# Routed experts in a transformer layer: picking by an added mask and a maximum, instead of weighing and summing

## The reference

```python
gates = jax.nn.softmax(xf @ wg, axis=-1)
idx = jnp.argmax(gates, axis=-1)
mask1 = jax.nn.one_hot(idx, E, dtype=x.dtype)
loc = jnp.sum((jnp.cumsum(mask1, 0) - 1.0) * mask1, -1).astype(jnp.int32)
keep = loc < cap
h = jnp.einsum('ecd,edf->ecf', disp, w1) + b1[:, None, :]
y = (jnp.einsum('ecf,efd->ecd', h, w2) + b2[:, None, :]).reshape(E * cap, D)
out = jnp.where(keep[:, None], gate_val[:, None] * y[jnp.minimum(slot, E * cap - 1)], 0.0)
```

## Time and profile before

| what | value |
| --- | --- |
| median of 3 runs | 667.09 us (665.74 to 670.02) |
| the profiled execution's own time | 663.18 us |
| its span, first to last instruction | 661.5 us |
| busy in the span: PE, DVE, ACT, POOL | 525.5, 543.0, 424.8, 229.2 us |
| mean granted TensorE clock | 0.911 |

### The profile page before, as it was taken

One profiled execution on the slowest core, in us unless ns is written; L12 is line 12 of the kernel. 1 busy time (PEld: TensorE's weight loads), 2 busy tenths in 40 slices (PEclk: granted clock), 3 DMA queues, 4 the chain that ended last, 5 costly groups with the idle time before them and its releaser, 6 DMA issues.

```text
span 661.5 us, 9881 instructions
## 1 busy us (share of the span) xinstructions
PE 525.5 (79%) x3439; PEld 208.4 (31%) x3439; DVE 543.0 (82%) x872; ACT 424.8 (64%) x909; POOL 229.2 (35%) x360
## 2 busy tenths in 40 slices
PE   2884799999899999999999986776486675998710
PEld 1570122222222222222222222555466542443300
DVE  4759799999899999999999933798838257899996
ACT  1542489989889888898889873434344403656554
POOL 7000110110133451334513480482344402686761
PEclk9996699999999999999999999887678686999955
DMA  9832011101211112111112001100000000000112
GB/s 247 256 130 113 16 34 26 41 26 46 60 56 39 30 41 63 57 35 34 47 53 60 14 6 27 56 1 1 0 1 1 1 1 0 0 1 0 33 32 63
DMA packets 31285, 28.92 MB, mean 44 GB/s; under 512 B 6132, under 2 KB 23676, under 8 KB 31236
## 3 DMA queue, kind: packets, MB, share of 16 engines
q1 hardware_dynamic: 29204, 27.31, 14.2%
q10 hardware_dynamic: 2032, 0.98, 0.6%
HBM read 19.23 MB, written 8.65 MB: 42 GB/s over the span
## 4 chain that ended last, share of the span: by engine, by line
PE 45%; DVE 27%; POOL 10%; ACT 10%; issue 4%; DMA 3%; SPq 1%; ACTq 0%; DVEq 0%; POOLq 0%
PE ps L1293 13%; PE ps L1288 10%; DVE row_max L1465 8%; PE ps L1261 5%; PE ps L620 3%; DVE space L898 2%; DVE st L241 2%; PE ps L605 2%; ACT attended L1413 2%; ACT space L1397 2%; DMA space<-max_turned 1%; DVE space L889 1%; DVE space L776 1%; DVE space L264 1%; DMA w_in<-in_L_ffn_out_proj_w 1%
## 5 line engine op out<-in xcount | busy, mean ns | idle before, releaser
L1465 DVE TENSOR_REDUCE row_max<-ps 128x2 f32<-128x1024 f32 x256 | 299.6, 1219 | 17.3 <-PE ps L1261 14.4
L1397 ACT ACTIVATE space<-ps 128x512 f32<-128x512 f32 x512 | 271.9, 605 | 48.6 <-PE ps L1288 48.2
L1288 PE MATMUL ps<-space 51*128 51x512 bf16 x512 | 158.0, 385 | 9.4 <-DMA space<-max_turned 5.2
L1293 PE MATMUL ps<-space 128*32 128x512 f32 x1024 | 137.0, 607 | 3.0 <-ACT space L1397 0.7
L1261 PE MATMUL ps<-space 48*128 48x512 bf16 x512 | 127.6, 398 | 14.2 <-DVE row_max L1465 12.6
L1163 POOL CAST max_parts<-row_max 128x16 bf16<-128x16 f32 x32 | 6.3, 196 | 269.0 <-DVE row_max L1465 269.0
L1288 PEld LDWEIGHTS ps<-space 51*128 51x128 bf16 x512 | 40.7, 94 | 167.3 <-ACT space L1397 145.8
L620 PE MATMUL ps<-W,space 128*128 128x512 f32 x128 | 70.6, 634 | 0.0
L428 POOL TENSOR_TENSOR space<-PC,same_row 128x512 f32<-128x512 f32 x32 | 32.9, 1059 | 60.0 <-DVE PC L792 60.0
L734 ACT ACTIVATE space<-ps,weight 128x128 f32<-128x128 f32 x128 | 34.3, 382 | 20.8 <-PE ps L620 9.3
L1261 PEld LDWEIGHTS ps<-space 48*128 48x128 bf16 x512 | 26.3, 94 | 55.0 <-DVE row_max L1465 49.5
(11 more groups left out here) (201 smaller groups left out, 697.1 us busy)
## 6 DMA issues: line engine op xcount, KB each, us to landing
q_parts_dram<-space SPq DMA_DIRECT2D x2, 1536.0 KB, 5.4
space<-q_parts_dram SPq DMA_DIRECT2D x64, 48.0 KB
attended_dram<-attended SPq DMA_DIRECT2D x128, 18.0 KB
X<-in_L_attn_queries SPq DMA_DIRECT2D x8, 256.0 KB, 7.5
space<-in_L_ffn_w SPq DMA_DIRECT2D x2, 1024.0 KB, 5.9
space<-q_parts_dram SPq DMA_DIRECT2D x64, 32.0 KB
space<-attended_dram SPq DMA_DIRECT2D x16, 128.0 KB, 2.4
space<-inverses_dram SPq DMA_DIRECT2D x16, 128.0 KB
```

Of the source, the lines that this page charges most:

```text
L1288: pe.matmul(ps[:, col_bank(v), :], k_rows[rows_a, kappa // 4 % 2, tc * P:(tc + 1) * P], q_stack[rows_a, kappa % 4, b * S:(b + 1) * S], sta ...
L1293: mm = pe.matmul(ps[32 * m:32 * m + 32, PV, :], v_heads[:, tc, PAIR * (kappa // 4) + m % PAIR, :], probs[:, tc % 2, m, :], start=(tc == 0) ...
L1397: act.activation(probs[:, tc % 2, m, :], ps[:, col_bank(v), :], ACT.Exp, scale=1.0 / math.sqrt(DH)).then_inc(s_pr, 1)
L1465: dve.tensor_reduce(row_max[:, par].rearrange("p (a c) -> p a c", a=PAIR)[:, :, item], ring(n), AX.X, MAX).then_inc(s_free, 1)
```

## The change

*Picking.* `W` is stored with the expert as its innermost index, so a tile's 1024 columns are 128 features of 8 experts each. PE adds to them, by one product with 32 rows of a mask, the bias rows and -1e30 for each expert that was not chosen; DVE takes the maximum over the eight (`select`, 1024 to 128). This needs only the group's own choice (`choose`, the steps of L842 to L851 on 64 columns), turned by PE (`turn_mask`) and inverted by DVE (`copy_others`), and not the places; so the tiles no longer wait for the routing of all tokens. The gate value is applied later to 128 features (`weigh`: DVE for groups 0 and 3, ACT for 1 and 2 with a sum on POOL).

*The softmax steps.* `scores2` first adds -1e30 to the pairs that don't belong together (four products over 512 columns, one on each strip of 32 rows), and DVE takes a maximum over 16 straight from PSUM in place of L776 and L779.

*The order.* Groups 0 and 1 (tiles 0 to 15) are computed between the softmax steps 4 to 7, all in the one PSUM pair of banks 6 and 7; tile k+1 waits until tile k is selected. Group 2 (tiles 16 to 23) stands around the last group's norm and routing, in a ring of three pairs. Only group 3 is left behind the routing (`last_tile`).

*The rest.* The `c_stack` loads move out of the place ahead of `load_shift(0)` into slots 2 to 5 of the loop (16 DMAs for 4), and POOL builds the masks in slots 1 to 8. ACT copies the attended values with one instruction for four.

The core of the diff:

```diff
-ACT_WEIGHS, POOL_SUMS = [0, 2, 4, 6], [0, 3, 5, 6]
...
+BIG = 1e30
+RING = [0, 2, 4]
+EARLY = 2 * B
...
-        W = sb("W", [P, E, D])
+        W = sb("W", [P, D, E])
...
+            def sum_up(g):
+                pool.wait_ge(s_wa, g)
+                pool.tensor_tensor(same(A[:, g]), same(A[:, g]), same(YT[:, g]), ADD).then_inc(s_sum, 1)
...
-        EXPERT_BANKS = [4, 6, 2, 0]
+        def expert_bank(k):
+
+            return 6 if k < EARLY else RING[(k - EARLY) % len(RING)]
...
+                for h in range(NH2):
+                    rows_h = slice(HD2 * h, HD2 * h + HD2)
+                    pe.matmul(ps[:, h, :], own_row[rows_h, :],
+                              other_row[rows_h, :].rearrange("p (o f) -> p o f", o=1).broadcast_to([HD2, 4, P]),
+                              start=True, stop=False)
...
+            def experts(k):
+
+                g, b = k // B, k % B
+                bank, rows_k, variant = expert_bank(k), slice(32 * (b // 2), 32 * (b // 2) + 32), b % 2
+                for half in range(2):
+                    cols = slice(half * 512, half * 512 + 512)
+                    pe.matmul(ps[:, bank + half, :], others[rows_k, g, :], c_stack[rows_k, variant, cols],
+                              start=True, stop=False)
+                    mm = pe.matmul(ps[:, bank + half, :], YT[:, g, b, :], W[:].rearrange("p d e -> p (d e)")[:, cols],
+                                   start=False, stop=True)
+                mm.then_inc(s_xp, 1)
...
+            pe.wait_ge(s_cb, QB)
+            for q in range(2 * QPG, 2 * G):
+                g, half, k = q // QPG, q % QPG, 4 * (q - 2 * QPG)
+                pe.wait_ge(s_ot, q)
+                if q == 4:
+                    pe.wait_ge(s_lgc, 1)
+                if q == 6:
+                    pe.wait_ge(s_nm, 2)
+                spread_turned(q, 0, 4)
+                if q == 4:
+                    pe.wait_ge(s_res, 2)
+                    turn_mask(0)
+                if half == 1:
+                    pe.wait_ge(s_sel, k)
+                    turn_y1(g - 1)
+                pe.wait_ge(s_et, 2 * q + 1)
+                spread_turned(q, 1, 4)
+                if half == 0:
+                    pe.wait_ge(s_res, g)
+                    pe.wait_ge(s_nm, g - 1)
+                else:
+                    pe.wait_ge(s_y1c, 2 * g)
+                experts(k)
+                if q != 4 and q + 2 < 2 * G:
                     scores2(q + 2)
+                pe.wait_ge(s_sel, k + 1)
+                experts(k + 1)
+                attend(q)
+                if q == 4:
+                    pe.wait_ge(s_ot, q + 1)
+                    pe.wait_ge(s_sel, k + 2)
+                    turn_tokens(3)
+                    project(3)
+                    pe.wait_ge(s_qkv, 3 * G)
+                    scores2(6)
                 if half == 1:
+                    route(g - 1)
+                pe.wait_ge(s_sel, k + 2)
+                experts(k + 2)
+                pe.wait_ge(s_sel, k + 3)
+                experts(k + 3)
+                if half == 1:
+                    turn_mask(g - 1)
+                    pe.wait_ge(s_sel, k + 4)
+                    project_out(g)
...
+            for k in range(EARLY, EARLY + B):
+                if k - EARLY >= len(RING):
+                    pe.wait_ge(s_sel, k - len(RING) + 1)
+                experts(k)
...
+            def weigh(g):
+                act.wait_ge(s_sel, B * (g + 1))
+                for b in range(B):
+                    ins = act.activation(YT[:, g, b, :], YT[:, g, b, :], ACT.Copy, scale=gate[:, B * g + b:B * g + b + 1])
...
-                dve.tensor_tensor(SM[:], ps[:, 0:4, :].rearrange("p a (t f) -> p (a t) f", f=P),
-                                  bcast(same_row[:], 16), MUL).then_inc(s_msk, 1)
+                dve.tensor_reduce(SC[:, q].rearrange("p a m -> p (a m)"),
+                                  ps[:, 0:4, :].rearrange("p a (t n) -> p (a t) n", n=16), AX.X, MAX).then_inc(s_msk, 1)
...
-                ch.done(dve.tensor_reduce(SC[:, q], SM[:].rearrange("p a (m n) -> p a m n", n=16), AX.X, ADD))
...
+            def copy_others(g):
+                dve.wait_ge(s_mt, g + 1)
+                dve.tensor_scalar(others[:, g, :], turned_mask(g), -1.0, 1.0, MUL, ADD).then_inc(s_nm, 1)
+
+            def select(k):
+
+                bank = expert_bank(k)
+                dve.wait_ge(s_xp, k + 1)
+                dve.tensor_reduce(YT[:, k // B, k % B, :], ps[:, bank:bank + 2, :].rearrange("p a (d e) -> p (a d) e", e=E),
+                                  AX.X, MAX).then_inc(s_sel, 1)
...
+            residual(0)
+            ln1(0)
+            compact(4)
+            normalise(4)
...
             ch.done(norm(dve, ch, LAST1, tiles(A, last), tiles(A, last)))
...
+            choose(0)
...
             norm(dve, ch, LAST2, tiles(X, last), tiles(A, last)).then_inc(s_n2l, 1)
+            residual(1)
+            copy_others(0)
+            compact(5)
+            normalise(5)
+            select(0)
+            ln1(1)
+            for k in range(1, 4):
+                select(k)
+            compact(6)
+            normalise(6)
+            select(4)
+            select(5)
+            choose(1)
+            select(6)
+            select(7)
+            copy_others(1)
+            residual(2)
+            compact(7)
+            normalise(7)
+            select(8)
+            ln1(2)
+            for k in range(9, 14):
+                select(k)
+            choose(2)
+            select(14)
+            select(15)
+            copy_others(2)
...
+            def last_tile(b):
+                k = (G - 1) * B + b
+                select(k)
+                dve.wait_ge(s_sel, k + 1)
+                ch.done(weigh(k))
...
-                dve.tensor_tensor(A[:, g, b, :], A[:, g, b, :], e_sum[:, DVE_SUMS.index(b)], ADD).then_inc(s_sv, 1)
+                ch.done(dve.bn_stats(st64(G - 1)[:, b, :], A[:, G - 1, b, :]))
...
+            variance4(0)
+            last_tile(0)
+            scale4(0)
+            last_tile(1)
+            dve.wait_ge(s_sum, 1)
+            variance4(1)
...
-            sp.wait_ge(s_csplit, 1)
-            c_rows = c_stack[0:PARTS, :].rearrange("q (r j d) -> q r j d", r=2, d=D)
-            for j in range(E2):
-                sp.dma_start(c_rows[:, :, j, :], c_parts[32 * j:32 * j + 1]).then_inc(s_cl, 16)
...
+                if 2 <= kappa < 2 + QB:
+                    load_c(kappa - 2)
```

More of the change, by code:

```diff
@@ L28 @@
 KALL = KROWS + PARTS
-KPAD = 96
 EPS = 1e-5
@@ new lines, in back_end_pe @@
+            turn_mask(G - 1)
+            pe.wait_ge(s_lgc, G)
+            masks = maskp[:].rearrange("p g k c -> p (g k) c")[:, :, MASK_ROW:MASK_ROW + 2 * E]
+            pe.matmul(ps[:, 6, 0:T * E], upper[:], masks, start=True, stop=True)
+            pe.matmul(ps[:, 6, T * E:2 * T * E], all_ones[:], masks, start=True, stop=True).then_inc(s_cnt, 1)
+            pe.wait_ge(s_nm, G)
+            for k in range(EARLY + B, T):
+                pe.wait_ge(s_sel, k - len(RING) + 1)
+                experts(k)
@@ new lines, in back_end_act @@
+            root(act, LAST1)
+            copy_logits(0)
+            copy_turned(4, 0, 4)
+            root(act, LAST2)
+            copy_turned(4, 1, 4)
+            softmax_exp(5)
+            copy_attended(4)
+            root(act, LN1[1])
+            copy_tokens(3)
+            project(3)
+            copy_turned(5, 0, 4)
+            copy_y1(1, 6)
+            copy_turned(5, 1, 4)
+            softmax_exp(6)
+            copy_attended(5)
+            copy_logits(1)
+            copy_turned(6, 0, 4)
@@ L956, in back_end_dve @@
-            variance5(g - 1, True)
-            variance4(g)
-            scale5(g - 1)
+            for b in range(B):
+                ins = weigh(b)
+            ch.done(ins)
+            ch.wait()
+            variance4(0)
[4 more added lines that the diff above has]
+            variance4(1)
+            last_tile(2)
+            last_tile(3)
+            scale4(1)
+            last_tile(4)
+            last_tile(5)
+            variance5(0)
@@ L959, in back_end_dve @@
+            last_tile(6)
+            scale5(0)
+            last_tile(7)
+            dve.wait_ge(s_sum, 2)
+            variance4(2)
+            scale4(2)
+            variance5(1)
+            scale5(1)
+            variance5(2)
+            scale5(2)
+            g, odd = G - 1, range(1, B, 2)
+            dve.wait_ge(s_n4, 2)
+            ch.wait()
+            norm_smalls(dve, ch, st64(g), small4(g))
             scale4(g)
-            ch.done(norm_apply(dve, tiles(A, g), tiles(A, g), small, odd))
+            ch.done(norm_apply(dve, tiles(A, g), tiles(A, g), small4(g), odd))
```

560 lines of the change are left out of this document (270 added, 290 removed).

## The result

The changed kernel takes 708.87 us (median of 4 runs, 706.68 to 711.12), where the kernel before takes 667.8 beside it: the ratio is 1.0615, with a 95% interval of 1.0565 to 1.0664. It is 6% slower. The forecast was 673.6 us in a range of 655 to 688.

The account below looks back on a forecast made before the run. No engine full in softmax steps and norms; DVE and PE nearly full in the experts' stage. Terms -1.6 - 3.6 + 27.6 + 24.5 + 4.8 - 45.2 = +6.5 us on 661.5; as median 673.6 us, range 655 to 688.

Parts of the forecast that it names:

- Start of the loop, -1.6: Loop start: without four DMAs ahead, the shift lands about 2.6 us earlier and PE starts at 72.95, saving 1.6 us.
- Softmax steps, -3.6: Up to residual 1: DVE loses a 2.29 us pass per step, PE gains four products; residual 1 comes 3.6 us earlier.
- Tiles 0 to 15, +27.6 and +24.5: Between softmax steps: one bank pair makes PE and DVE alternate, adding 27.6 us (residual 1 to 2) and 24.5 (2 to 3).
- the walk: Step-by-step timing of the engines' programs through the whole kernel, with tile rounds of 3.67 us; chance 0.6 for 661 to 684.
- the tiles cool PE: Rival in tiles 0 to 15: 2.3 us work and 1.3 pause per round halve the clock; 698 us, chance 0.15.
- Faster: the tiles fit in the gaps: Rival before routing: tile rounds run beside other work, each saving 3.67 us; four give 659 us, chance 0.2.
- Select reads slowly: Rival in the selects: reading eight neighbours takes 1.93 us instead of 1.22, adding 17 us; 691 us, chance 0.05.
- Routing, +4.8: Residual 3 to the gate: less DVE work but eight tiles and selects beside it, 28.7 us instead of 23.9.
- Behind the gate, -45.2: Gate to end: eight last tiles 26.7 us, last group's scale at 45.5, then 15.6; 61.1 us instead of 106.3.
- What would show it: Signs of a right forecast: first column scores near 73 us, select 1.22, gate near 607, 61 us from gate to end.
- three marks for "wrong": Signs against the forecast: gate before 595 or beyond 620 us, tail above 66 us, or clock of 0.5 in tile rounds.
- DVE's wait ahead of tile 2: Before tile 2: DVE idle some 11 us, released by PE behind ACT's last copy of the projection.

Follow-up runs that it names:

- rows32_before: The kernel before with the product that adds the constants cut from 96 rows to 32: 677.28 us, ratio 1.0151.
- keep_busy: The changed kernel with products that nobody reads put into PE's waits: 699.77 us, ratio 1.0494 to the kernel before.
- rows_longer_pause: full_rows with a DVE clearing of some 0.5 us ahead of each of selects 0 to 15: 691.46 us, ratio 1.0353 to the kernel before.
- full_rows: The changed kernel with each tile's mask product on all 128 rows instead of 32, zeros outside its own: 684.17 us, ratio 1.0269 to the kernel before.
- after: The changed kernel itself, without any follow-up edit, as profiled: 708.87 us, ratio 1.0615 to the kernel before.

## Why the prediction was wrong

*Start of the loop, -1.6.* Right: the first column scores start at 72.5 us (74.5 before), 2.1 us earlier, and no longer wait for a DMA.

*Softmax steps, -3.6.* Not refuted. Residual 1 was forecast at 473.8 and stands at 473.4 to 478.0 in the eight profiles of kernels with this front, 477.3 in the changed kernel's own. The front of before varies too: 479.0 in its profile and 481.6 in that of `rows32_before`. The means, 476.4 and 480.3, are 3.9 us apart where 5.2 were forecast. The four added products were priced right: at full clock they take 0.39 us, and the scores start 0.23 us behind their start (0.3 forecast).

*Tiles 0 to 15, +27.6 and +24.5: the step that failed.* It said that a tile alone on a warm PE takes 2.33 us, and took this from the earlier trace rows, whose first product is on 96 rows. The changed one is on 32, and that was read in the diff and not priced. A tile costs 2.75 us at full clock and 5.08 at the lower one (2 x 2.54 in the rows above), where the kernel before, with 96 rows, took 2.16 and 4.24. The two stretches took 68.7 and 58.7 us. With that product on 128 rows, and 2 us of extra copies, they took 58.8 and 45.6, against 58.2 and 46.2 forecast; the walk itself, with its rounds of 3.67 (3.64 measured), was right to 1 us.

The Trainium skill has the rule ("TensorEngine Tiling (Array Packing)", Key Properties): changing the tiling mode drains TensorE. The trace agrees as far as it goes, with 1.37 against 1.08 us a half tile in the otherwise same kernel (`rows32_before`); a drain as such is not seen in it. The prediction did not weigh the rule.

*The clock.* The rival "the tiles cool PE" had 0.15 at 698 us and came true in part: by `keep_busy` the cold in the waits that it fills costs about 9 us. Its reason, pauses and DVE's norms between, was not enough, as `rows_longer_pause` shows. The argument from the earlier trace rows, that pauses of this size leave the clock at 1.00, came from products on 96 and 128 rows, held for 128-row ones in `rows_longer_pause`, and was carried over to 32-row ones. Both errors thus come from the same 32 rows: 25 us together by the medians of `full_rows`, 27 by the spans.

*Faster: the tiles fit in the gaps.* No: with full rows both stretches last what the walk gives with its rounds on the path. *Select reads slowly*: no, 1.22 us.

*Routing, +4.8.* 30.8 us instead of 28.7; 28.1 with full rows.

*Behind the gate, -45.2: the second step that failed.* It summed DVE's operations at their lengths from rows where POOL was quiet, and gave 61.1 us. It put POOL's passes on the chain at 2.36 us and looked no further. What POOL did to DVE is worth more than the passes themselves: without them DVE is busy for 15.4 us less and the stretch takes 57.9 us. So the walk was 3.2 us too long for a stage in which POOL disturbs nobody, and the 15.9 us that POOL's passes cost were missing: +12.7 in all. The text gives 26.7 us for the eight last tiles and 45.5 at the last scale, but not all terms of the two, so which of them was too long stays open. And the trace of before had the price: L250 at 452.87 us and L255 at 617.93, in the lines above, last 2.2 us instead of 0.17, each under a pass of POOL's.

The Trainium skill ("SBUF — State Buffer", Who interferes with whom) says that a DVE instruction with two SBUF inputs contends with a GpSimd instruction that reads SBUF. One with at most one does not, outside the modes in which DVE uses both ports, and `tensor_scalar` is among those that can enter such a mode. The traces agree. With two inputs, L250, L254 and L257 last 2.2 us under POOL's passes. With one, the reciprocal lasts 0.20 us under a pass, and the `tensor_scalar` L255 of the kernel before 2.28 us. In which mode that one ran the trace doesn't say.

*What would show it.* The gate stood at 635.5 us, beyond 620, the tail (from the gate to the end) at 73.8, above 66, and the clock was 0.5 in tile rounds: all three marks for "wrong" were met. The first was to mean clock or `select`, and the longer products were not among its causes. DVE's wait ahead of tile 2 was put at some 11 us, though the terms of the text (10.0 + 1.6 + 2.33) give 14; it was 15.9, and 15.4 in `full_rows`.

In all, the change made the stretch from the gate to the end 32.5 us shorter (106.3 to 73.8), and the stretch from residual 1 to the gate 82.0 us longer (76.2 to 158.2).

## What to carry to other kernels

A product copied from a trace is a price only for the same number of rows: mixing 32-row and 128-row products costs 0.3 to 0.4 us for each pair of changes, and padding the small one with zeros to 128 rows cost nothing on PE (and some 2 us of copies on DVE here). Work moved into another engine's gaps should be able to run ahead; with one pair of banks each tile puts PE's and DVE's time one after the other, and the same tiles behind the steps, in three pairs and with full rows, made the kernel 3.4% faster than before. And where DVE does many small operations, look at what POOL runs beside them, in the trace of before already.

## What the runs showed of the hardware

- A 32-row product (bf16, 512 columns) between 128-row ones lengthens the half tile from 1.08 to 1.37 us at the upper clock and to 2.54 us at the lower, where the kernel before, with 96 rows, took 2.13. With both narrow ones in front a tile takes 2.35 instead of 2.75 us.
- In rounds of a product group and a wait, the clock fell to 0.50 in some with 32-row products among them (2.7 of 4 us busy in the step before, `after`) and stayed at 1.00 with 128-row ones (2.2 of 4 us busy, `rows_longer_pause`). In an unbroken row of tiles the 32-row products left it at 1.00 (`rows32_before`).
- A DVE operation on 8 columns with two SBUF inputs, started under a POOL pass of 2.34 us, took up to 2.25 us, and DVE counts as busy meanwhile: 15.4 us in one stage of 73.8. A `tensor_scalar` with one input was held too (2.28 us, kernel before), a reciprocal was not (0.20 us).
